# Cross attention on one Trainium2 core: unit splits behind the last turn, the last batch's tokens loaded twice, eight projections inside the self-attention, join and norms in pieces

## The reference

```python
def _mha(q_in, k_in, v_in, Wq, Wk, Wv, bv, causal):      # 16 heads of 32
    q = jnp.einsum('bsd,hde->bhse', q_in, Wq)
    k = jnp.einsum('btd,hde->bhte', k_in, Wk)
    v = jnp.einsum('btd,hde->bhte', v_in, Wv) + bv[None, :, None, :]
    scores = jnp.einsum('bhse,bhte->bhst', q, k) * scale
    ...
    p = jax.nn.softmax(scores, axis=-1)
    o = jnp.einsum('bhst,bhte->bhse', p, v)
...
sa = _mha(x, x, x, Wq1, Wk1, Wv1, bv1, causal=True)
x = _layernorm(sa + input_tensor, g1, be1)
ca = _mha(x, encoder_output, encoder_output, Wq2, Wk2, Wv2, bv2, causal=False)
x = _layernorm(x + ca, g2, be2)
ffn = jax.nn.relu(x @ Wf1 + bf1) @ Wf2 + bf2
x = _layernorm(x + ffn, g3, be3)
...
x = x + _L0_xattn_ref(_layernorm(x, axis=-1), ctx_1024, ...)
x = x + _L0_attn_ref(_layernorm(x, axis=-1), ...)
x = x + _L0_ffn_ref(_layernorm(x, axis=-1), ...)
```

## Time and profile before

| | us |
|---|---|
| median of three executions | 1624.4 |
| lowest, highest | 1619.35, 1627.89 |
| the profiled execution: its time, its span | 1628.24, 1626.8 |
| busy: PE | 1495.2 (92% of the span) |
| busy: DVE, ACT, POOL | 907.5, 668.8, 256.0 |
| POOL's 44 subtractions of L549 | 158.9, mean 3.613 |
| one subtraction over 128x2048 on DVE (L1636, in the experts) | mean 2.284 |

### The profile page before, as it was taken

One profiled execution on the slowest core, in us unless ns is written; L12 is line 12 of the kernel. 1 busy time (PEld: TensorE's weight loads), 2 busy tenths in 40 slices (PEclk: granted clock), 3 DMA queues, 4 the chain that ended last, 5 costly groups with the idle time before them and its releaser, 6 DMA issues.

```text
span 1626.8 us, 28472 instructions
## 1 busy us (share of the span) xinstructions
PE 1495.2 (92%) x12052; PEld 1149.4 (71%) x12052; DVE 907.5 (56%) x1338; ACT 668.8 (41%) x1217; POOL 256.0 (16%) x171
## 2 busy tenths in 40 slices
PE   7799999999999999999988877968997799999998
PEld 3479888877787878778777665853597476666665
DVE  3633423544535354454465435357677478888886
ACT  1424432443444344334345433423321246666664
POOL 1213211110201010211121415020252100000000
PEclk9889999999999999999999987988888789999999
DMA  7013110110101010101111345032000029999992
GB/s 245 2 43 95 59 43 21 43 40 21 43 21 43 21 40 27 37 27 37 40 43 40 105 180 182 1 124 108 1 1 27 0 104 338 345 346 343 344 340 90
DMA packets 86780, 163.15 MB, mean 100 GB/s; under 512 B 4608, under 2 KB 27136, under 8 KB 86144
## 3 DMA queue, kind: packets, MB, share of 16 engines
q1 hardware_dynamic: 86656, 161.34, 28.7%
HBM read 160.28 MB, written 1.05 MB: 99 GB/s over the span
## 4 chain that ended last, share of the span: by engine, by line
PE 86%; DVE 9%; issue 2%; ACT 1%; POOL 1%; DMA 0%; ACTq 0%; DVEq 0%
PE ring L591 18%; PE ring L581 16%; PE ring L1787 8%; PE turnbank L625 6%; PE pv L1811 4%; PE sc L608 3%; PE pv L644 3%; PE sc L1065 3%; PE sc L1452 3%; PE pv L1787 3%; PE pv L1819 2%; PE sc L1475 1%; PE ring L1074 1%; PE pv L653 1%; DVE nm L813 1%
## 5 line engine op out<-in xcount | busy, mean ns | idle before, releaser
L549 POOL TENSOR_TENSOR x_l<-raw,x_h 128x1536 fp32r<-128x1536 f32 (+1 forms) x44 | 158.9, 3613 | 739.5 <-ACT x_h L543 739.5
L1636 DVE TENSOR_TENSOR w_lo<-w_raw,w_hi 128x2048 fp32r<-128x2048 f32 x88 | 200.4, 2284 | 25.1 <-ACT w_hi L1877 25.0
L731 ACT ACTIVATE prob<-sc,nm 128x384 f32<-128x384 f32 (+1 forms) x256 | 153.9, 611 | 119.5 <-DVE nm L818 80.6
L581 PE MATMUL ring<-x_h,wk_h 128*128 128x384 f32 (+1 forms) x512 | 186.5, 364 | 5.4 <-POOL x_l L549 5.4
L591 PE MATMUL ring<-wv_h,x_h 128*128 128x512 f32 (+2 forms) x520 | 191.4, 368 | 0.0
L813 DVE TENSOR_REDUCE nm<-sc 128x2 f32<-128x898 f32 (+1 forms) x128 | 127.9, 1020 | 105.1 <-PE sc L608 105.0
L591 PE MATMUL ring<-wv_h,x_l 128*128 128x512 f32 (+2 forms) x520 | 181.4, 349 | 0.0
L591 PE MATMUL ring<-wv_l,x_h 128*128 128x512 f32 (+2 forms) x520 | 181.1, 348 | 0.0
L581 PE MATMUL ring<-x_h,wk_l 128*128 128x384 f32 (+1 forms) x512 | 177.2, 346 | 0.0
L581 PE MATMUL ring<-x_l,wk_h 128*128 128x384 f32 (+1 forms) x512 | 176.8, 345 | 0.0
L1877 ACT CAST w_hi<-w_raw 128x2048 fp32r<-128x2048 f32 x88 | 167.6, 1907 | 18.4 <-PE pv L1811 15.5
(11 more groups left out here) (450 smaller groups left out, 2643.9 us busy)
## 6 DMA issues: line engine op xcount, KB each, us to landing
w_raw<-in_ew SPq DMA_DIRECT2D x96, 1024.0 KB, 5.5
raw<-in_ctxT SPq DMA_DIRECT2D x33, 768.0 KB, 4.3
...
```

Source lines behind the costliest of these rows:

```text
L549: pool.tensor_tensor(x_l[x % 3][:, :, 0:w], raw[x % 3][:, :, 0:w], x_h[x % 2][:, :, 0:w].bitcast(F32), ALU.subtract)\
L581: m = pe.matmul(ring[k % 2][:, 0:w], wt[:, c, e:e + P], xt[:, c, 0:w], start=c == 0 and n == 0, stop=c == NC - 1 and n == 2)
L731: act.activation(prob[:, i, 0:WIDTHS[r]], sc[:, i, score_columns(r)], ACT.Exp, bias=nm[:, b % 2, r, h:h + 1], accum_out=psum[:, b % 2, r, ...
L1636: return eng.tensor_tensor(w_lo[n % NSLOT][:, :, :], w_raw[n % NSLOT][:, :, :], w_hi[i % 4][:, :, :].bitcast(F32), ALU.subtract)
```

## The change

1. **Self-attention.** `EARLY` has eight jobs instead of three. Two follow each token block on PE, their copies follow the block's work on ACT and DVE. As they use `ring`, the next block's turn waits for both copies (`pe_copied`).
2. **Splits.** `act_splits_behind`: the cast of a unit is issued behind the last turned copy of the following iteration, ahead of that iteration's exponentials.
3. **Tokens.** In the last batch, the first three head blocks' jobs of half 0 run in rounds 48 to 55 (25 jobs, were 21), the rest in rounds 56 to 60 (17, were 21). The tokens are loaded twice where they were loaded three times: 40 units instead of 44.
4. **Banks.** From turn 1 of round 62 on, turns rotate over `turnbank`, `ring[0]` and `ring[1]`.
5. **Join.** It is split: factors and scale in iteration 8b, add in 8b+1. For the last batch, groups 0 to 2 are joined before the last fold and group 3 behind it. The bias `bv2` is added once for all blocks by POOL at the start of the cross attention.
6. **Norms.** The norm of the X_B blocks is in two pieces at other places; in the FFN it comes ahead of the splits of the weights, and the first hidden block waits chunk by chunk. At the end of the FFN `be3` is added to the residual beforehand (one 128x2048 DVE operation), and the last norm's application moves from DVE to ACT, with a third small POOL operation per block.

```diff
@@ -284,7 +285,7 @@
             normalised(t)
-        dve_jobs(dve, EARLY)
+            dve_jobs(dve, EARLY[2 * t:2 * t + 2])
@@ -324,11 +325,11 @@
                 exponentials(t + 2)
-        act_jobs(act, EARLY[:1])
+            act_jobs(act, EARLY[2 * t:2 * t + 2])
             act.copy(nT[:, c, :], bank[c]).then_inc(sem("turned_copied"), 1)
-        act_jobs(act, EARLY[1:])
+        act_splits_behind(act, EARLY)
@@ -370,6 +371,7 @@
                 pe.wait_ge(sem("probs_copied"), 2 * t)
+                pe_copied(pe, 2 * t - 1)
@@ -404,16 +406,15 @@
             outputs(t)
-        pe.wait_ge(sem("split_low"), 2)
-        for k in EARLY[:2]:
-            pe_project(pe, k)
+            if t == 0:
+                pe.wait_ge(sem("split_low"), 2)
+            for k in EARLY[2 * t:2 * t + 2]:
+                pe_project(pe, k)
         m.then_inc(sem("turned"), 1)
-        for k in EARLY[2:]:
-            pe_project(pe, k)
@@ -455,16 +456,13 @@
     ALL = range(len(VTILES))
-    FAR = [i for i in ALL if VTILES[i][0] == 0]
-    NEAR = [i for i in ALL if VTILES[i][0] == 1]
         segment(b, range(NC), None, ALL, range(8 * b - 8, 8 * b))
-    segment(B - 1, (0, 1), 0, ALL, range(8 * B - 16, 8 * B - 8))
-    segment(B - 1, (2,), 1, FAR, range(8 * B - 8, 8 * B - 5))
-    segment(B - 1, (3,), 1, NEAR, range(8 * B - 5, 8 * B - 3))
+    segment(B - 1, (0, 1, 2), 0, ALL, range(8 * B - 16, 8 * B - 8))
+    segment(B - 1, (3,), 1, ALL, range(8 * B - 8, 8 * B - 3))
@@ -479,7 +477,7 @@
-    EARLY = range(3)
+    EARLY = range(8)
@@ -503,6 +501,11 @@
         return sum(1 for m, j in TURNS[:turn_index(n, k) + 1] if turn_owner(m, j) == owner)
+    FREE = turn_index(8 * B - 2, 0)
+    def turned_bank(i):
+        return (turnbank, ring[0], ring[1])[(i - FREE) % 3 if i > FREE else 0]
@@ -550,6 +553,10 @@
     def pool_cross(pool, link):
+        pool.wait_ge(sem("rows_loaded"), 64)
+        pool.wait_ge(sem("turned"), 2)
+        pool.tensor_tensor(xa[:, :, :], xa[:, :, :], over_tiles(bv2[:, :]), ALU.add).then_inc(sem("bias_added"), 1)
+        pool.wait_ge(sem("bias_added"), 1)
@@ -616,13 +623,15 @@
         i = turn_index(n, k)
-        if i > 0:
-            m, j = TURNS[i - 1]
+        if i in (FREE + 1, FREE + 2):
+            pe_copied(pe, NJ - 1)
+        elif i > 0:
+            m, j = TURNS[i - 3 if i > FREE else i - 1]
             t0, w = tiles[t]
-            m = pe.transpose(turnbank[0:w, s * P:(s + 1) * P], prob[:, head, t0:t0 + w], ident[:, :])
+            m = pe.transpose(turned_bank(i)[0:w, s * P:(s + 1) * P], prob[:, head, t0:t0 + w], ident[:, :])
@@ -655,11 +664,9 @@
     def pe_cross(pe):
-        for k in range(len(EARLY), LAST_JOB[0] + 2):
-            pe_project(pe, k)
         for x in (1, 2, 3):
-            for k in range(max(LAST_JOB[0] + 2, LAST_JOB[x - 1] + 1), LAST_JOB[x] + 1):
+            for k in range(max(len(EARLY), LAST_JOB[x - 1] + 1), LAST_JOB[x] + 1):
@@ -710,6 +717,10 @@
                 act.copy(dst, src).then_inc(sem("job_copied_a"), 1)
+    def act_splits_behind(act, jobs):
+        for k in jobs:
@@ -749,26 +760,25 @@
     def act_cross(act):
-        for x in (0, 1, 2, 3):
...
+        for i in range(4):
+            act_exp(act, 0, i)
+        for x in (1, 2, 3):
+            jobs = range(max(len(EARLY), LAST_JOB[x - 1] + 1), LAST_JOB[x] + 1)
+            act_jobs(act, jobs)
+            act_splits_behind(act, jobs)
             act_turned(act, n, last_turn(n))
+            if n > 0:
+                for s in range(slots_of(n - 1)):
+                    act_splits_behind(act, PLAN[n - 1][s])
                 act_exp(act, n + 1, 1)
+            else:
+                act_join(act, B - 1)
@@ -776,6 +786,8 @@
                 act_exp(act, n + 1, 3)
+            if n % 8 == 0 and n > 0:
+                act_join(act, n // 8 - 1)
@@ -824,18 +834,22 @@
+    def dve_denominators(dve, link, g):
...
+    def dve_mix(dve, link, g):
...
@@ -858,68 +872,75 @@
...
+    def dve_join_scale(dve, link, b, groups):
...
+    def dve_join_add(dve, link, b, groups):
...
+        if b == 0:
+            dve.wait_ge(sem("bias_added"), 1)
+        return dve.tensor_tensor(xa[r, t, cols], xa[r, t, cols], cat[r, cols], ALU.add)
         dve.memset(sc[S:P, :, FIRST[1] + W0:512], MASKED).then_inc(sem("pad_masked"), 1)
-        for x in (0, 1, 2, 3):
...
+        dve_max(dve, link, 0)
+        for x in (1, 2, 3):
+            dve_jobs(dve, range(max(len(EARLY), LAST_JOB[x - 1] + 1), LAST_JOB[x] + 1))
             more, b = n + 1 < NR, n // 8
-            joins = n % 8 == 0 and n > 0
+            joins, every = n % 8 < 2 and n >= 8, range(0, 4)
             dve_jobs(dve, PLAN[n][0])
-            if joins:
-                dve_join_factors(dve, link, b - 1)
-            if n % 2:
+            if joins and n % 2:
+                dve_join_add(dve, link, b - 1, every).then_inc(sem("cross_added"), 1)
+            if n == NR - 1:
+                dve_denominators(dve, link, n // 2)
+                dve_join_factors(dve, link, b)
+                dve_join_scale(dve, link, b, range(0, 3))
+                link(dve_join_add(dve, link, b, range(0, 3)))
                 dve_mix(dve, link, n // 2)
-            elif more:
+            elif n % 2:
+                dve_denominators(dve, link, n // 2)
+                dve_mix(dve, link, n // 2)
+            else:
                 dve_turned(dve, n + 1, 0)
-            if joins:
-                dve_join_scale(dve, link, b - 1)
                 dve_turned(dve, n + 1, 1)
-            if joins:
-                dve_join_add(dve, link, b - 1)
+            if joins and n % 2 == 0:
+                dve_join_factors(dve, link, b - 1)
+            if n in X_B:
+                dve_x_b_stats(dve, link, X_B.index(n))
                 dve_turned(dve, n + 1, 2)
+            if n in X_B:
+                dve_x_b_center(dve, link, X_B.index(n))
+            if joins and n % 2 == 0:
+                dve_join_scale(dve, link, b - 1, every)
             dve_jobs(dve, PLAN[n][3])
-            if n % 8 == 7:
+            if n % 8 == 7 and more or n == NR - 2:
                 dve_join_shift(dve, link, b)
-            if n in X_B:
-                dve_x_b(dve, link, X_B.index(n))
                 dve_x_b_end(dve, X_B.index(n - 1))
-        dve_join_factors(dve, link, B - 1)
-        dve_join_scale(dve, link, B - 1)
-        dve_join_add(dve, link, B - 1)
+        dve_join_scale(dve, link, B - 1, range(3, 4))
+        dve_join_add(dve, link, B - 1, range(3, 4)).then_inc(sem("cross_added"), 1)
@@ -981,13 +1002,15 @@
-    def dve_x_b(dve, link, t):
+    def dve_x_b_stats(dve, link, t):
             dve.wait_ge(sem("rows2_loaded"), 32)
-        link(dve.tensor_tensor(xa[:, t, :], xa[:, t, :], bv2[:, :], ALU.add))
         norm_stats(dve, link, xa, t)
+    def dve_x_b_center(dve, link, t):
@@ -1001,10 +1024,11 @@
+        dve_x_b_stats(dve, link, NT - 1)
+        dve_x_b_center(dve, link, NT - 1)
+        dve_x_b_end(dve, NT - 1)
         split(1)
-        dve_x_b(dve, link, NT - 1)
-        dve_x_b_end(dve, NT - 1)
@@ -1014,6 +1038,7 @@
         link(dve.tensor_tensor(xa[:, :, :], xa[:, :, :], over_tiles(bf2[:, :]), ALU.add))
+        link(dve.tensor_tensor(xres[:, :, :], xres[:, :, :], over_tiles(rows3[:, 1, :]), ALU.add))
@@ -1022,14 +1047,9 @@
             link(norm_center(dve, tmp, t, rows3[:, 0, :]))
-        for t in range(NT + 1):
-            if t < NT:
-                link(norm_shift(dve, 3, tmp, tmp, t, rows3[:, 1, :]))
-                link(dve.tensor_tensor(xa[:, t, :], tmp[:, t, :], xres[:, t, :], ALU.add))
-                norm_stats(dve, link, xa, t)
-            if t >= 1:
-                norm_apply(dve, 4, tmp, xa, t - 1).then_inc(sem("normed"), 1)
+        for t in range(NT):
+            link(norm_shift(dve, 3, xa, tmp, t, xres[:, t, :]))
+            norm_stats(dve, link, xa, t)
@@ -1054,13 +1074,21 @@
+    def act_last_norm(act):
+        for t in range(NT):
+            act.wait_ge(sem("shift_scaled"), t + 1)
+            act.activation(tmp[:, t, :], xa[:, t, :], ACT.Identity, scale=rstd[:, t:t + 1], bias=nshift[:, t:t + 1])\
+               .then_inc(sem("normed"), 1)
         pe_turn(pe, xa, 2)
-        pe.wait_ge(sem("turned_copied"), 12)
             for c in range(NC):
+                if m == 0:
+                    pe.wait_ge(sem("turned_copied"), 8 + c + 1)
@@ -1197,9 +1225,13 @@
     def pool_delta(pool, link):
-        for n in (3, 4):
-            for t in range(NT):
-                norm_rstd(pool, link, n, t)
+        for t in range(NT):
+            norm_rstd(pool, link, 3, t)
+        for t in range(NT):
+            norm_rstd(pool, link, 4, t)
+            pool.wait_ge(sem("rstd_ready"), norm_count(4, t))
+            pool.tensor_scalar(nshift[:, t:t + 1], mv[:, t, 0:1], rstd[:, t:t + 1], -1.0, ALU.mult, ALU.mult)\
+                .then_inc(sem("shift_scaled"), 1)
```

(48 more changed lines are left out.)

11 lines of the change are left out of this document (5 added, 6 removed).

## The result

The change makes the kernel slower, by 1.8%. The changed kernel took 1654.89 us (median of four runs, 1649.18 to 1660.29) against 1626.14 before (four runs, 1619.35 to 1628.03): ratio 1.0184, 95% interval 1.0131 to 1.0237. The direction was forecast, the size was not: +17 was forecast (1641, with a range of its own of 1632 to 1650), about +29 came between the medians. The profiled execution took 1659.23 with a span of 1657.7, 30.9 above the span before.

What follows compares the result with a forecast made beforehand. PE was taken to pace the rounds, DVE the self-attention, a serial chain the stretch from round 62. Terms 6 + 17 + 8 + 0 - 12.5 - 1.5 = +17 on 1624.4 gave 1641 (1632 to 1650; with rivals 1593 to 1655).

Steps and rivals of the forecast that it cites:

- The mechanism: Rounds 0 to 47: POOL's subtraction starts 0.10 us ahead of DVE's small maximum and blocks it, delaying PE's turn; +17.
- The clock term: Rounds 0 to 47: half of ten new PE gaps drop the clock, 1.65 us each; +8 (0 to 16).
- The iteration 8b+8: Each batch's last cast in rounds 0 to 47: slot 0 holds two jobs, leaving about 0.4 us idle.
- C: Last batch, rounds 48 to 60: two waits for POOL go, blocked maxima replace them; 0 (-12 to +5).
- D: Round 62 to the first hidden block: three banks, shorter join and earlier norm; -12.5 (-10 to -14).
- A: Self-attention with eight jobs: turns wait for the odd job's copy at three seams; +6 (3 to 9).
- E: Last norms: DVE loses an operation and an add per block, POOL becomes the chain; -1.5 (-2.5 to +0.5).
- Rival 1: Splits in the rounds: DVE is first, only the second maximum is blocked; -24, so 1600; chance 0.28.
- Rival 2: Splits in the rounds: maxima blocked but the clock holds; +6, 1630, no difference; chance 0.20.
- Rival 3: All blocked, every gap drops the clock, self-attention seams at upper bound; another +14, 1655; chance 0.10.

Runs made afterwards that it cites:

- e1_delay: Changed kernel with one small ACT copy ahead of each cast from round 1 on; 1651.91 us, ratio 1.0177.
- e5_delay_more: Changed kernel with four small ACT copies ahead of each cast; 1613.03 us, ratio 0.9917.
- e7: Changed kernel with part 1 undone, three early jobs instead of eight; 1652.70 us, ratio 1.0157.
- e8: Changed kernel with the be3 add behind the FFN's weight splits instead of ahead of the third; 1652.96 us, ratio 1.0160.
- e9: Kernel before the change with only the casts moved behind the last turned copy, in rounds 0 to 47; 1656.60 us, ratio 1.0212.
- The filler: Changed kernel with 16 extra PE transposes ahead of turn 0: in every iteration behind a cast 1659.58 us; only where PE stood idle 1644.33 us.
- e10: Changed kernel with inline casts and the last batch's segments as before, tokens loaded three times; 1625.52 us, ratio 1.0014.
- e3: Changed kernel with the casts of the rounds inline again, right behind a unit's last job; 1603.61 us, ratio 0.9878.

## Why the prediction was wrong, step by step

**The mechanism was right.** POOL's 0.10 of lead, the length of the block, the 2.36 and 2.0 before turn 0, and that only the second maximum is blocked behind the 1800-wide cast: all as forecast. The Trainium skill ("SBUF — State Buffer", section "Who interferes with whom"), cited in the prediction, says that whoever issues first keeps the shared ports for its whole length; e1_delay and e5_delay_more show it to a hundredth of a microsecond. No record shows a shared pace: the blocked maximum ends with POOL's subtraction, whose 1536-wide records stay between 3.4 and 3.53 us. The 16 long records of the kernel before are the same thing; the prediction spoke of five or so among 128 records, and there are 64. Its reading of the page ended too early as well, without effect: PE's slices below 9 run on to the 32nd, with three nines among them.

**The clock term was too small, and it is the largest miss.** The step that failed is "I take half of them": five falls, +8. The clock fell behind seven of the ten waits in this trace, each time at 1.7: 11.9 us. It fell behind ten of ten in e7, nine of ten in e8, eight of ten in e9 and eight of nine in e1: 42 of 49 in the five traces. In the last batch the forecast had 1.6 more for the clock than before (3.3 less 1.7), and 3.4 came: four falls against two. Behind the wait ahead of the first down product the clock fell once more, 1.7, for which there was no term. Together these are 7.4 of the 13.9 us by which the profiled execution came out above +17. The rows I had (a fall behind 1.97, none behind 1.62) already said that waits of 2.0 and 2.4 lie on the falling side; I halved them for the busy PE around, for which no row spoke. The filler, which keeps PE at work, is the proof that the idle time itself is the cause.

**PE's busy time** rose by 3.1 beyond the falls in rounds 9 to 48. The forecast had nothing for it, and its cause stays open.

**The iteration 8b+8 was taken at 0.4.** There two jobs hide the blocked maximum, but small waits stay around it: 0.33 twice and 0.49 in rounds 33 and 34 and in rounds 17 and 18, 1.15 in all, and 0.55 to 0.6 in the other three batches. With the five waits of 0.78 to 1.12 at turn 1 (0.9 forecast) the idle time is +19.3 instead of +17.

**C** came out at +1.5 against 0, inside its bounds, as two large numbers. The segments were worth -16 (e10 against e3: 11.1 less idle, 5.1 less for the clock), which I had as 5.4 of waits, 1.7 of clock and a share of the rest. The blocked maxima took it back: +14.8 (the changed kernel against e3: 8.0 of idle, 6.8 of clock), where I had 13.6. Two slips stand in the working: the idle time of the two stretches is 11.46 + 8.71 = 20.2, not 19.2, and the clock fell behind both waits of the earlier trace rows, which is 3.4 and not 1.7.

**D** was right to the first hidden block (-13.0 against -13.8), and short behind it. Outputs(63) come 6.0 earlier after round 62's scores (5.9 forecast); how the rest divides between the join and the order of the norm, no run shows, as parts 4 to 6 were not undone one by one there. The be3 add delays the down product by its whole 2.3 and not by 1.3, and this wait drops the clock: another 1.7 which the forecast didn't have. e8_be3_late gives both back.

**A** (+5.4, 6 forecast) was right, its seams too: the self-attention's last norm ends at 107.20 instead of 94.74, +12.5 where 13 was forecast. It comes with a scatter that I had put in its bounds: round 1 stands at offsets from +3.1 to +8.0 in the traces that share this part. **E** was -2.9 against -1.5.

Rival 1 did not happen, but e5_delay_more is its case: DVE is first. It took 1613, 14 below the kernel before on its chip, where I had worked out -24 and 1600. The largest part of that difference is the rounds up to 48: +1.4 from round 1, where I had -4, with waits of 1.15 and 1.49 behind the 1800-wide casts. The last batch gives 3.1 of it (-8.9 from 48 to 62, where I had -12), the FFN 1.9. Rival 2 was excluded by the PEclk of 0.72. Rival 3 came nearest in time (1655), by its clock term. That it meets the measured 1654.89 so closely is luck: it counts +3 for seams that didn't come and every gap as a fall, and has nothing for the FFN's clock and the busy time.

What stays open is why the clock falls behind some waits of one length and not behind others of the same: behind the same iteration 14 it held in one trace and fell in another. Once it fell where no single wait was long: in e10_inline_old_segments, at 863.5, where waits of 1.51 and 1.01 stand close together. The spread of the changed kernel's four runs (11 us) goes with the clock: their mean granted clocks are 0.951 and 0.953 in the two longer ones, 0.955 and 0.957 in the two shorter ones, and 0.006 of 1650 us is 10.
